# A lookup-and-interaction tower: eleven fields looked up by one-hot matmuls instead of thirteen, fifteen gathered, and the order of the later stages changed

## The reference

```python
e = jnp.stack([tbl_0[ids[:, 0]], ..., tbl_25[ids[:, 25]]], axis=1)
T = jnp.concatenate([dense[:, None, :], embs], axis=1)
Z = jnp.einsum('bnd,bmd->bnm', T, T)
z = Z[:, iu0, iu1]                       # pairs n < m
h = jnp.concatenate([z, r_dense], axis=1)
h = jnp.maximum(h @ W_top1 + b_top1, 0.0)   # 479 -> 512
h = jnp.maximum(h @ W_top2 + b_top2, 0.0)   # 512 -> 256
y = h @ W_top3                              # 256 -> 1
```

## Time and profile before

| | |
|---|---|
| median of 3 runs | 129.84 us (129.02 to 130.34) |
| the profiled execution's own time | 131.07 us |
| its span, first to last instruction | 129.2 us |
| busy PE / DVE / ACT / POOL | 109.3 / 86.0 / 77.2 / 68.4 us |
| first one-hot matmul | 6.47 us |
| tables 0 to 10 done, tile 2's first group transposed | 60.73 us |
| table 12 done, first product | 78.05, 79.73 us |
| tile 3's first product | 110.33 us |
| last copy of `y` starts | 127.47 us |

### The profile page before, as it was taken

The page is one execution under the profiler, slowest core; times in us unless marked ns, Lnnn a source line. Parts: engine busy times, 40 slices in busy tenths (PEclk is TensorE's granted clock), DMA queues, the critical chain, the costliest instruction groups (busy, mean ns, idle before and its releaser), DMA issues.

```text
span 129.2 us, 2741 instructions
## 1 busy us (share of the span) xinstructions
PE 109.3 (85%) x1032; PEld 92.8 (72%) x1032; DVE 86.0 (67%) x211; ACT 77.2 (60%) x166; POOL 68.4 (53%) x62
## 2 busy tenths in 40 slices
PE   5895799999993999999029996865879999999992
PEld 5863678788672888777027875865868997899980
DVE  4398889998988489979602666699423962295211
ACT  3383988996994987997105655699301944392001
POOL 2678888888888789889877778740000000003000
PEclk9999999999999999999976999999999999999999
DMA  4989967868867847579941212120000000000000
GB/s 107 238 240 284 316 217 255 235 215 274 295 210 163 257 110 240 147 256 217 393 131 41 61 41 61 46 73 12 16 8 0 10 16 3 5 0 21 5 0 0
DMA packets 7819, 16.86 MB, mean 130 GB/s; under 512 B 2466, under 2 KB 3390, under 8 KB 7678
## 3 DMA queue, kind: packets, MB, share of 16 engines
q1 hardware_dynamic: 5934, 13.06, 33.6%
q0 software_dynamic: 1728, 3.43, 9.4%
q10 hardware_dynamic: 144, 0.20, 0.5%
HBM read 16.44 MB, written 0.00 MB: 127 GB/s over the span
## 4 chain that ended last, share of the span: by engine, by line
PE 37%; POOL 36%; issue 9%; DMA 9%; DVE 4%; SPq 3%; ACT 1%; DVEq 0%; ACTq 0%
POOL rows L331 36%; PE work L398 8%; PE work L348 7%; PE work L442 6%; DMA rows<-tbl,idx 5%; PE work L380 4%; PE work L382 4%; PE work L342 3%; SPq L269 2%; DMA idx<-ids 2%; PE work L450 2%; PE tp L366 2%; DMA Zt<-Zlow 1%; DVE Zt L470 1%; DVE Zlow L463 1%
## 5 line engine op out<-in xcount | busy, mean ns | idle before, releaser
L331 POOL DMA_INDIRECT rows<-tbl,idx x52 | 66.5, 1278 | 18.0 <-issue 15.5
L593 DVE TENSOR_SCALAR hot<-ids_bc,rownum 128x512 fp32r<-128x512 int32 x95 | 41.0, 489 | 15.7 <-PE work L382 13.1
L380 PE MATMUL work<-hot,t_hi 128*128 128x512 f32 x118 | 48.3, 409 | 3.0 <-ACT hot L510 2.3
L382 PE MATMUL work<-hot,t_lo 128*128 128x512 f32 x118 | 46.7, 396 | 0.0
L380 PEld LDWEIGHTS work<-hot,t_hi 128*128 128x128 f32 x118 | 22.6, 191 | 10.9 <-ACT hot L510 4.4
L382 PEld LDWEIGHTS work<-hot,t_lo 128*128 128x128 f32 x118 | 22.6, 192 | 4.2
L578 DVE TENSOR_TENSOR t_lo<-table,t_hi 128x1280 fp32r<-128x1280 f32 (+3 forms) x15 | 17.9, 1198 | 0.6 <-ACT t_hi L483 0.6
L483 ACT CAST t_hi<-table 128x1280 fp32r<-128x1280 f32 (+3 forms) x15 | 15.4, 1028 | 4.6 <-DMA table<-small 4.6
L398 PE MATMUL work<-XT 128*64 128x52 f32 x512 | 16.2, 222 | 2.3 <-DVE Zt L470 1.3
L398 PEld LDWEIGHTS work<-XT 128*64 128x64 f32 x512 | 15.5, 138 | 3.3 <-issue 1.7
L500 ACT ACTIVATE apart<-ids_bc,minus_row 128x512 f32<-128x512 int32 x23 | 16.4, 715 | 1.9 <-DMA ids_bc<-ids_oh 1.9
(11 more groups left out here) (34 smaller groups left out, 61.7 us busy)
## 6 DMA issues: line engine op xcount, KB each, us to landing
table<-small SPq DMA_DIRECT2D x7, 640.0 KB, 4.8
ids_bc<-ids_oh SPq DMA_DIRECT2D x13, 256.0 KB, 4.1
table<-small SPq DMA_DIRECT2D x4, 512.0 KB, 3.7
w_sb<-w SPq DMA_DIRECT2D x1, 1024.0 KB, 8.0
rows<-tbl,idx POOLq DMA_INDIRECT x52, 4.0
table<-small SPq DMA_DIRECT2D x2, 320.0 KB, 5.1
w_sb<-w SPq DMA_DIRECT2D x1, 512.0 KB, 8.1
dense_t<-dense SPq DMA_DIRECT2D x1, 256.0 KB, 5.5
```

What stands on the lines that cost most here:

```text
L331: nc.gpsimd.indirect_dma_start(rows[:, t, place - FIRST, :], None, tbls[f], bass.IndirectOffsetOnAxis(ap=idx[:, t, f:f + 1], axis=0)).then ...
L380: nc.tensor.matmul(bank, t_hi[:, i % PARTS, c * D:(c + 1) * D], hot[:, k % HOTS, :], start=c == 0, stop=False)
L382: last = nc.tensor.matmul(bank, t_lo[:, i % PARTS, c * D:(c + 1) * D], hot[:, k % HOTS, :], start=False, stop=c == n - 1)
L593: nc.vector.tensor_scalar(hot[:, k % HOTS, :], ids_bc[:, i % IDS, :], rownum[:, v, c:c + 1], None, ALU.is_equal).then_inc(hot_dve, 1)
```

## The change

- `ONEHOT` loses two tables of 10 chunks: 11 tables, 98 chunks. Fifteen fields are gathered: 60 gathers, in groups of 4, 4, 4 and 3. All ids come in one DMA, in the order in which they are used.
- ACT copies each table by itself (128x512, `copy_lookups`), and table 10 in two parts; six banks of `work` go round.
- POOL's gathers now wait (`row_turn`): gather j (from 0) for 3j-14 chunks of the lookup, and from 39 on for steps of PE.
- DVE clears `XT`'s padding at its start; dense is loaded behind table 5 and copied behind table 8. DVE makes the first low part ahead of the first one-hot.
- Rows: tile 0 after tables 3, 5 and 6, tile 1 after 7, 8 and 10, tile 2 between the products of tiles 0 and 1 and the layers of tile 0. "layer1" of tile 2 stands ahead of the last row group of tile 3.
- "dense" t, four matmuls, is a step of its own ahead of the wait for the moves.
- Layer 2 of tiles 0 to 2 has `h1` as the stationary operand, samples on partitions: 4 matmuls of 256 columns; DVE adds the bias (`TENSOR_TENSOR`) and one `SCALAR_TENSOR_TENSOR` takes max, times `w3`, and sums into `y_column`. Their "layer3" goes. Tile 3 keeps its layer 2 and 3.
- In tile 3 the second product's low pairs are copied ahead of the first one's last high pairs, and POOL moves three of the four low pieces.

```diff
-ONEHOT = [4, 5, 6, 12, 16, 23, 2, 9, 11, 13, 14, 15, 18]
+ONEHOT = [4, 5, 6, 12, 16, 23, 2, 9, 11, 13, 14]
+CHUNKS_PER_ROW = 3
+CHUNKS_BEHIND = 14
+GRAMS_FIRST = {39: 1, 40: 2, 42: 3, 44: 4, 54: 5, 55: 6}
+TILE_ROWS_FIRST = {46: (2, 1), 50: (2, 2), 52: (2, 3), 59: (3, 0)}
+LAYER1_FIRST = {48: 1, 49: 2, 57: 3, 58: 4}
+LAYER2_FIRST = {51: 1}
-SHARED_MOVES = 2
+SHARED_MOVES = 3
+            def row_turn(j):
+                if 0 < chunks_first(j) and chunks_first(j - 1) < first_hot(K_OH):
+                    pool.wait_ge(hot_used, groups_used(chunks_first(j)))
+                if j in GRAMS_FIRST:
+                    pool.wait_ge(gram_full, GRAMS_FIRST[j])
...
+            def copy_lookups(i):
+                act.wait_ge(hot_used, groups_used(first_hot(i + 1)))
...
+                    nc.scalar.copy(XT[:, :, 1 + i], lookup_bank(i)).then_inc(lookup_copied, 1)
...
-                        first = LOOKUPS * lookup_group(i)
-                        nc.scalar.copy(XT[:, :, 1 + first:2 + i],
-                                       lookup_banks(i).rearrange("p f b -> p b f")).then_inc(lookup_copied, 1)
...
+                    for u in range(BLOCKS):
+                        last = nc.tensor.matmul(l2_block(t, 0), h1[:, u, :], w2_sb[:, u, :], start=u == 0,
+                                                stop=u == BLOCKS - 1)
...
+                    nc.vector.tensor_tensor(h2_sum_sb[:], l2_block(t, 0), ends_sb[:, 0, :], ALU.add).then_inc(h2_sum, 1)
+                    dve.wait_ge(h2_sum, t + 1)
+                    nc.vector.scalar_tensor_tensor(out=h2_part[:], in0=h2_sum_sb[:], scalar=0.0, in1=ends_sb[:, 1, :],
+                                                   op0=ALU.max, op1=ALU.mult,
+                                                   accum_out=y_column[:, t:t + 1]).then_inc(y_ready, 1)
```

More of the change, by code:

```diff
@@ L80 @@
 COUPLE = 2
+COUPLED = PAD + FIELDS
 GRAM_BANKS = 4
@@ L169, in hots_made, with dlrm_tower @@
     return sum(by_scalar(x) == scalar for x in range(k + 1))
-def dlrm_tower(nc, dense, ids, ids_oh, tbls, small, w1, w2, tail, out):
+def dlrm_tower(nc, dense, ids, ids_oh, tbls, small, w1, w2, tail, ends, out):
     f32, f32r, i32 = mybir.dt.float32, mybir.dt.float32r, mybir.dt.int32
@@ L524, in _ @@
                 if kind == "onehot":
-                    for k in mine_in(i)[1:]:
+                    for n, k in enumerate(mine_in(i)[1:]):
                         one_hot(k)
+                        if n == 0 and i:
+                            copy_lookups(i - 1)
+                    if i and len(mine_in(i)) < 2:
+                        copy_lookups(i - 1)
                     if i + 2 < K_OH:
@@ L541, in _ @@
                     act.wait_ge(gram_full, halves + 1)
-                    copy_gram(nc.scalar.copy, t, i, halves % HALVES,
-                              range(SAMPLES - ACT_SAMPLES, SAMPLES), low_act).then_inc(gram_act, 1)
+                    first, second = range(SAMPLES - ACT_SAMPLES, SAMPLES)
+                    copy_low(nc.scalar.copy, t, i, halves % HALVES, first)
+                    copy_low(nc.scalar.copy, t, i, halves % HALVES, second).then_inc(low_act, 1)
+                    if t == TILES - 1 and i == 1:
+                        copy_high(nc.scalar.copy, t, 0, (halves - 1) % HALVES, second).then_inc(gram_act, 1)
+                    copy_high(nc.scalar.copy, t, i, halves % HALVES, first)
+                    if t < TILES - 1 or i == 1:
+                        copy_high(nc.scalar.copy, t, i, halves % HALVES, second).then_inc(gram_act, 1)
                     halves += 1
@@ L566, in _ @@
             halves = 0
+            nc.vector.memset(XT[:, :, PLACES:PAD], 0.0).then_inc(xt_ready, 1)
             dve.wait_ge(iota_ready, len(KINDS))
@@ L604, in _ @@
                     dve.wait_ge(gram_full, halves + 1)
[L605 to L606 removed]
+                    first, second = range(SAMPLES - ACT_SAMPLES)
+                    copy_low(nc.vector.tensor_copy, t, i, halves % HALVES, first)
+                    copy_low(nc.vector.tensor_copy, t, i, halves % HALVES, second).then_inc(low_dve, 1)
+                    if t == TILES - 1 and i == 1:
+                        copy_high(nc.vector.tensor_copy, t, 0, (halves - 1) % HALVES, second).then_inc(gram_dve, 1)
+                    copy_high(nc.vector.tensor_copy, t, i, halves % HALVES, first)
+                    if t < TILES - 1 or i == 1:
+                        copy_high(nc.vector.tensor_copy, t, i, halves % HALVES, second).then_inc(gram_dve, 1)
                     halves += 1
[L608 removed]
+                elif kind == "layer1" and i == (1 if t < TILES - 1 else 0):
                     if t:
@@ L670 @@
     dlrm_tower(nc, aps["dense"], aps["ids"], aps["ids_oh"], {f: aps[f"tbl_{f}"] for f in GATHERED},
-               [aps[f"small_{i}"] for i in range(K_OH)], aps["w1"], aps["w2"], aps["tail"], out)
+               [aps[f"small_{i}"] for i in range(K_OH)], aps["w1"], aps["w2"], aps["tail"], aps["ends"], out)
     r = run(nc, [arrays], core_ids=[0])
```

231 lines of the change are left out of this document (123 added, 108 removed).

## The result

| | before | after |
|---|---|---|
| median, same chip | 130.09 us (129.02 to 131.19, 4 runs) | 120.84 us (119.67 to 124.03, 4 runs) |
| ratio, 95% interval | | 0.9238 (0.912 to 0.9357) |
| profiled execution, its span | 131.07, 129.2 us | 124.03, 120.6 us |
| first product | 79.73 us | 64.94 us |
| tile 3's first product (called T below) | 110.33 us | 103.07 us |

The change is worth 7.6%. Forecast were 113.0 us (13%) and a range of 110.5 to 117.5; the direction was right, the size was not, and the time lies above the range.

What follows compares the result with a forecast made beforehand. Two clocks were taken to bound it, PE's one-hot matmuls and POOL's gathers, with gathers leading (0.55). 96.2 (tile 3's product) + 8.7 + 5.7 + 1.8 = 112.4; + 1.87 - 1.23 = 113.0 us, range 110.5 to 117.5.

Steps and rivals of the forecast that it cites:

- The new `SCALAR_TENSOR_TENSOR` also reads two operands from SBUF: DVE's layer 2: two of these ahead of gather 57 lengthen gathers by 0 to 1.2 us, taken as 0.4.
- A gather lands 2.6 us after its issue once the table loads are over: Behind the lookup: with gather 57 at 88.1, tile 3's third group lands at 90.7.
- The weights' load ... is over before the rows of tile 1 are wanted: Lookup: the weights' load of 8.0 us moves two tables forward without making tile 1's rows late.
- the 2.04 us that PE had waited at 41.19: Lookup: PE's wait for tile 1's rows goes, since the second group is wanted near 49; 2.04 us saved.
- The clock falls in the new waits: Rival, 0.11: PE's clock halves behind the 3.3 and 1.9 us waits, +1.6 a time: 114.6 to 116.2 us.
- a wait of 3.3 us at the third group: Ahead of tile 3's product: PE wants the third row group at 87.4, and it lands at 90.7.
- PE leads: Rival, 0.18: ACT's copies, the dense load or the start end the lookup at 62 to 64: 114 to 116 us.
- Slower gathers: Rival, 0.08: the 26 late gathers keep the lookup's pace, 1.5 us instead of 1.25: +6.5, 119.5 us.
- the end of the lookup: PE's one-hot matmuls with two tables fewer and tile 2's rows moved behind the first products: end at 58.3 us.
- gather 57: POOL: the gather that completes tile 3's third group, put at 88.1 us.
- T to the pairs: Tail, from tile 3's first product to its pairs: 8.7 us, 2.0 earlier than before.
- The waits of the gathers: POOL's new waits for PE: gather 10 is held 0.2 to 0.4 us, later ones not; 0.4 in all.

Runs made afterwards that it cites:

- e_nostore: Changed kernel without the column stores of tiles 0 to 2, whose results are not written out: 113.0 us, ratio 0.8579 to the kernel before.
- e_ylate: Changed kernel with its three column stores issued behind tile 3's last moves: 113.91 us, ratio 0.8763 to the kernel before.
- e_yrows: Changed kernel with the three result columns transposed on PE and stored late as three 512-byte rows in one DMA: 114.56 us, 0.869 of the kernel before.
- r_after: Changed kernel run again without edit, on the chip of the runs beside it: 118.93 us, 0.909 of the kernel before.
- e_rows9: Changed kernel with tile 1's second row group transposed behind table 9 instead of table 8: 121.4 us, ratio 0.9327 to the kernel before.
- e_wlate: Changed kernel with the weights' loads waiting until tile 1's second row group has landed: 119.0 us, ratio 0.9301 to the kernel before.
- e_noturn: `e_yrows` without the gathers' new waits for PE (`row_turn`): 115.03 us, ratio 0.886 to the kernel before.
- e_13: `e_noturn` with all 13 one-hot tables and 52 gathers as before: 118.93 us, ratio 0.9254 to the kernel before.
- e_best: `e_yrows` plus seven extra matmuls filling PE's wait for tile 3's moves: 114.07 us, ratio 0.8771 to the kernel before.

## Why the prediction was wrong, and where it was right

**The step that failed: the stores have no term in the sum.** The prediction follows the new layer 2 only on DVE ("The new `SCALAR_TENSOR_TENSOR` also reads two operands from SBUF") and adds 0.4 us to the gathers for it. That `y_column` then leaves the core by three DMAs on SP, the first at 77.5 to 83.5 us, in the middle of the gathers that its own sum says are the bound, is nowhere costed; only the moves' issues on SP and POOL are. The trace of before had no store in column form, so the cost was unknown, and what should have been done with it is to bound it. Measured: gathers land in 5.8 us instead of 2.6, over 8 to 10 us. The sum "A gather lands 2.6 us after its issue once the table loads are over" took a row of a quiet stretch for one in which new transfers are issued. With the stores out of the way it is 2.5, and the time is 113.0 (`e_nostore`), 113.9 (`e_ylate`) and 114.6 (`e_yrows`), for 113.0 predicted. The loss is made of a wait of 3.75 or 4.10 us, and of the half clock that follows (3.62 for 1.97 us of layer 2): 99.39 - 58.92 = 40.5 us from the first product to T, where the sum had 36.9 and `e_ylate` has 35.4.

**A second one, seen in one profile: the weights.** "The weights' load ... is over before the rows of tile 1 are wanted" looked at the last two groups, behind table 10. The second group is wanted at table 8, near 49, and its last gather was put at "near 40" by the sum; in the profile after it was issued at 43.84, behind gathers that took 2.28 and 3.48 us beside DVE's low parts, 0.3 us ahead of 1.5 MB of loads. I credited the 2.04 us that PE had waited at 41.19 as saved for good; it came back as 2.85 us, with half clock behind it. In the other profiles of the changed kernel's lookup gather 23 was issued at 39.9 to 43.3 us, no such wait is there, and the first product starts between 58.9 and 61.4. That the weights are what made it land late is read from the one trace; no experiment separated it.

**"The clock falls in the new waits"** had 0.11. It fell behind each wait of 2.69 us or more (2.69, 2.85, 3.75, 3.77, 4.10, 4.14, 4.15 us), so a wait of 3.3 us at the third group would probably have made it fall. The tail's wait for the moves, 1.76 to 1.93 us, went either way: the pairs behind it ran at reduced clock in the profile after, `r_after`, `e_rows9` and `e_wlate` (1.90, 1.76, 1.76, 1.93 us), and at full clock in `e_nostore`, `e_yrows`, `e_noturn`, `e_ylate` and `e_13` (1.87, three times 1.86, 1.78). Windows of `r_after` and of `e_ylate` over the same kind of place, the tail's pairs (busy time of PE, PEld, DVE, ACT, POOL; granted clock, DMA share, GB/s):

```profile
106.00:112.00 6.00, 4.24 (x24) 4.08 (x23) 1.96 (x9) 0.88 (x5) 0.46 (x1) 0.72 0.05 7
```

```profile
102.00:108.00 6.00, 5.03 (x43) 4.65 (x44) 1.18 (x5) 0.92 (x3) 0.00 (x0) 1.00 0.04 0
```

The prediction had the price right (1.6 a time; measured 4.54 - 2.7 = 1.8 in the tail), but weighed one wait at a time. The waits are bound together: what makes the rows late makes the clock fall. The rival was less a rival than a companion of every other one, and a sum in which a wait grows past 2 us should carry its clock with it. In the runs without early column stores the mean clock is 0.97 to 1.0; with them it is 0.94 to 0.986. The tail stays open: all four profiles in which it fell have an early column store, the five in which it held have none, yet what PE does ahead of the wait looks the same in both groups, and the waits are within 0.2 us of each other. It may be chance, for waits of this length go either way far ahead of any store, too. At the kernel's start PE waits about 2 us for ACT in every profile; the clock fell behind that wait in `e_yrows`, `e_noturn` and `e_nostore` (2.08, 1.89, 1.91 us) and held in the others (1.80 to 2.24 us). Windows behind it in `e_yrows` and in `e_ylate`:

```profile
13.80:17.20 3.40, 3.32 (x8) 2.64 (x9) 1.83 (x4) 3.37 (x6) 2.60 (x3) 0.50 0.88 308
```

```profile
13.70:17.20 3.50, 3.50 (x15) 2.91 (x16) 2.74 (x6) 3.47 (x5) 2.87 (x3) 1.00 0.83 290
```

**"PE leads" (0.18) did not happen.** ACT's single copies take 1.12 us each in the mean, above the upper bound of 1.02 that I gave from the earlier trace rows, and the lookup still ended at 58.06: the spare time of ACT did hide them, as taken. **"Slower gathers" (0.08)** did not happen as described either: from gather 34 on each takes 0.94 or 0.95 at POOL, 1.25 us from start to start, to the last one, in the profile of `r_after` as in that of after. It was their landing that was slow, not their issue, and I had priced only the issue. The prediction dismissed the case because "gathers beside product copies took 0.94 to the last", which is a row of POOL's and says nothing of the DMA engines. The two `SCALAR_TENSOR_TENSOR` that were given 0.4 us show no effect: no gather from the 34th on took longer.

**Right by the numbers:** in `r_after` the end of the lookup (58.06 for 58.3), the first product (58.92 for 59.3) and gather 57 (87.90 for 88.1), and T to the pairs (8.4 to 8.7 for 8.7). Some of this is luck: over the profiles of kernels with 11 tables the first product lies between 58.9 and 64.9 us and gather 57 between 86.6 and 92.0. With the stores repaired, T is 94.35, 95.37, 95.54 and 96.92 (`e_ylate`, `e_yrows`, `e_best`, `e_noturn`) for 96.2, but 99.40 in the profile of `e_nostore`, and PE's wait at the third group, 3.3 us in the sum, is 0.43 to 2.69 us: the gathers bind less than was summed. At the pairs the chain names SP's small move, not POOL's last, as releaser. The waits of the gathers, given 0.4, cost nothing that can be seen: in the profile after and in `r_after` POOL's idle time names PE only in its usual gaps of 0.30 us.

**The best version.** `e_ylate` at 113.91 us is 5 to 7 us faster than the changed kernel (118.93 and 120.84) and 16 faster than before, and differs from it in the place of three stores. Rows in place of columns at the end, and fillers in the tail, make no further difference that these runs can tell.

**What stays open.** Why 128 pieces of 4 bytes slow the packets behind them: the records show which packets and for how long, not where they wait. Whether a row store among the gathers would do the same. Why the medians of the changed kernel differ by 1.9 us between two chips while those of the kernel before differ by 0.8. And what decides whether the clock falls behind a wait of about 2 us.

## What to carry to other kernels

List every DMA that a change adds, by engine, time and the size of its pieces, and not only the compute that feeds it: a store of one number per partition may be nothing by its own record and still slow everything on the DMA engines for some 8 us, so put it behind the last transfer that somebody waits for. When a change moves rows or weights, look at what is issued within a microsecond of the *last* transfer of each group, at the time where the group is wanted, and not only at the groups at the end. And when a sum ends in a wait of more than about 2 us on TensorE, price the half clock behind it together with the wait.

## What the runs showed of the hardware that I had not expected

- A store of 128 pieces of 4 bytes to HBM: about three in ten of the gather packets behind it took 2.8 us in the median instead of 0.23, and gathers landed in 5.8 us instead of 2.6, over 8 to 10 us. A program packet took 6.69 us where others take about 1, and one issue of a low move 5.70 us beside it. In another run PE stood 4.15 us with nothing to wait for in the profile, by my reading because its instructions were late (not shown: the slow program packet of that run was in 3.8 us before PE went on). Three such stores in a row, with nothing gathered behind them, cost nothing that can be seen.
- A gather whose issue was 0.3 us ahead of 1.5 MB of loads landed in 7.63 us (one profile), for 4.9 us beside the tables' loads and 2.6 with nothing large in flight.
- TensorE's clock fell behind every wait of 2.69 us or more. Behind waits of 1.76 to 2.24 us it fell in some profiles and held in others, with lengths that overlap. The Trainium skill, TensorE: Matmul & The Clock Gate, "What's actually happening", says that the number of matmuls at half clock at a kernel's start varies from run to run; behind the waits of about 2 us here it varies likewise.
- ACT's copy of 512 columns of a one-hot result took 1.12 us in the mean with one field alone, for 1.45 us with three fields in one copy: a field alone costs three quarters of three together.
